# Cross-attention: four buffers of probabilities, V as a ring of tiles, four groups of products with V

## What is computed

```python
k = (key @ Wk.T + bk).reshape(b, lk, H, DH)      # key = value = the context, lk = 1601
v = (value @ Wv.T + bv).reshape(b, lk, H, DH)
q = (query @ Wq.T + bq).reshape(b, lq, H, DH)    # query = layernorm(x), lq = 64
score = jnp.einsum('bqhd,bkhd->bhqk', q, k) / jnp.sqrt(jnp.float32(DH))
...
score = score + jnp.where(valid, 0.0, NEG)[:, None, :, :]
attn = jax.nn.softmax(score, axis=-1)
ctx = jnp.einsum('bhqk,bkhd->bqhd', attn, v).reshape(b, lq, d)
```

## Time and profile before

| | |
|---|---|
| median of 3 runs | 1616.15 us (1612.69 to 1616.39) |
| profiled execution | 1616.18 us, span of its instructions 1614.4 us |
| mean granted TensorE clock | 0.948 of full speed |
| TensorE busy | 1415.4 us, 88% of the span |
| VectorE, ScalarE, GpSimd busy | 1066.6, 900.3, 851.0 us |
| one round of the loop, b = 1 to 29 | 36.32 us |

### The profile page before, as it was taken

The page is one execution under the profiler, slowest core; times in us unless marked ns, Lnnn a source line. Parts: engine busy times, 40 slices in busy tenths (PEclk is TensorE's granted clock), DMA queues, the critical chain, the costliest instruction groups (busy, mean ns, idle before and its releaser), DMA issues. The chain is left out here.

```text
span 1614.4 us, 55265 instructions
## 1 busy us (share of the span) xinstructions
PE 1415.4 (88%) x24351; PEld 983.9 (61%) x24351; DVE 1066.6 (66%) x1681; ACT 900.3 (56%) x1195; POOL 851.0 (53%) x560
## 2 busy tenths in 40 slices
PE   4689999999999999999999999999997686549408
PEld 2357777777767777777767777777775355324107
DVE  7756666666666666666666666666663768785984
ACT  2445566565565566565565566665565565425752
POOL 5567666665555666665555666665530698420000
PEclk9899999999999999999999999999998899679859
DMA  5564444444454444444444444444420521010001
GB/s 169 128 155 105 105 105 114 121 124 113 117 143 106 105 105 114 123 119 116 118 139 107 105 105 112 125 120 114 116 64 25 151 54 28 1 40 0 1 0 53
DMA packets 90495, 155.97 MB, mean 97 GB/s; under 512 B 16704, under 2 KB 55496, under 8 KB 90256
## 3 DMA queue, kind: packets, MB, share of 16 engines
q1 hardware_dynamic: 88256, 150.92, 35.7%
q10 hardware_dynamic: 2000, 1.51, 0.4%
HBM read 60.95 MB, written 2.20 MB: 39 GB/s over the span
## 5 line engine op out<-in xcount | busy, mean ns | idle before, releaser
L638 DVE TENSOR_REDUCE MXP<-W_PS 128x1 f32<-128x512 f32 x768 | 498.9, 687 | 283.8 <-PE W_PS L450 283.8
L534 ACT ACTIVATE PR<-S_PS 128x1024 f32<-128x1024 f32 (+1 forms) x416 | 424.9, 1023 | 259.1 <-PE S_PS L398 251.2
L344 POOL TENSOR_TENSOR K_HI<-K,MCOL 128x512 f16<-128x512 f32 (+1 forms) x224 | 219.5, 980 | 425.7 <-ACT K L542 424.5
L346 POOL TENSOR_TENSOR K_LO<-K,K_HI 128x512 f16<-128x512 f32 (+1 forms) x224 | 291.9, 1303 | 17.6
L450 PE MATMUL W_PS<-STK,QS 105*128 105x512 f16 (+1 forms) x1024 | 269.8, 335 | 8.8 <-POOL STK L371 4.8
L398 PE MATMUL S_PS<-QS,STK 105*128 105x128 f16 (+1 forms) x3328 | 256.1, 220 | 1.0 <-DVE QS L652 1.0
L413 PEld LDWEIGHTS O_PS<-PR,V 128*17 128x17 f32 x13312 | 191.1, 98 | 79.5 <-issue 59.4
L413 PE MATMUL O_PS<-PR,V 128*17 128x64 f32 x13312 | 231.5, 220 | 7.8 <-ACT PR L534 7.5
L433 PE MATMUL W_PS<-WV_HI,CTX_HI 128*128 128x256 f16 (+1 forms) x832 | 228.3, 274 | 1.6 <-DVE WV_LO L611 1.4
L398 PEld LDWEIGHTS S_PS<-QS,STK 105*128 105x128 f16 (+1 forms) x3328 | 201.3, 99 | 44.4 <-DVE QS L652 1.1
L433 PE MATMUL W_PS<-WV_HI,CTX_LO 128*128 128x256 f16 (+1 forms) x832 | 227.8, 274 | 0.0
(11 more groups left out here) (243 smaller groups left out, 1599.0 us busy)
## 6 DMA issues: line engine op xcount, KB each, us to landing
CTX<-in_ctx_t SPq DMA_DIRECT2D x64, 800.5 KB, 5.9
STK<-K_HI SPq DMA_DIRECT2D x256, 128.0 KB, 2.5
STK<-K_HI SPq DMA_DIRECT2D x256, 72.1 KB, 2.1
STK<-K_LO SPq DMA_DIRECT2D x128, 128.0 KB, 2.6
STK<-K_LO SPq DMA_DIRECT2D x128, 72.1 KB, 2.1
QSTK<-STK SPq DMA_DIRECT2D x12, 192.0 KB
SQS<-QK_HI SPq DMA_DIRECT2D x32, 64.0 KB, 2.2
X<-in_x SPq DMA_DIRECT2D x1, 1536.0 KB, 15.7
```

The source lines that it names most:

```text
L344: pool.tensor_tensor(K_HI[:, m, lo:hi], k32, zero, ALU.add).then_inc(k_hi, 1)
L346: pool.tensor_tensor(K_LO[:, m, lo:hi], k32, K_HI[:, m, lo:hi], ALU.subtract).then_inc(k_lo, 1)
L534: nc.scalar.activation(PR[0:m, par, :], S_PS[par][0:m, :], ACT.Exp).then_inc(p_sb, 1)
L638: dve.tensor_reduce(MXP[:, j, at:at + 1], bank[:, :], AX.X, ALU.max).then_inc(mx_done, 1)
```

## The change

PR gets four buffers instead of two, in turn over all tiles of all batches, so an exponential waits for the PV four before it. V becomes one array with room for 11 pairs of tiles, used as a ring: the copy of pair i of batch n waits until the PV of the pair that lay there have been done (`v_free`). The ring of K32 has three buffers instead of four. Some tiles that only the start uses move (XN to PR, KMH to other partitions of V). And SCHEDULE has another order, with the same steps: PV stand in four groups (0 to 3, 4 to 6, 7 and 8, 9 to 12) instead of seven, MX and V begin earlier in a round, OT and CH come later, and K 6 stands last. FIRST is unchanged.

```diff
@@ -61,20 +61,14 @@
 
 
 SCHEDULE = [
-    ("ST", 0), ("QS", 0), ("CH", 0), ("OT", 0), ("V", 0),
-    ("ST", 1), ("V", 1),
-    ("PV", 0), ("PV", 1), ("ST", 2), ("MX", 0), ("MX", 1), ("V", 2), ("MX", 2),
-    ("ST", 3), ("MX", 3), ("V", 3), ("MX", 4), ("MX", 5),
-    ("PV", 2), ("PV", 3), ("ST", 4), ("MX", 6), ("MX", 7), ("V", 4), ("MX", 8),
-    ("ST", 5), ("MX", 9), ("V", 5), ("MX", 10), ("MX", 11),
-    ("PV", 4), ("PV", 5), ("ST", 6), ("MX", 12), ("MX", 13), ("V", 6), ("MX", 14),
-    ("ST", 7), ("MX", 15), ("K", 0), ("MX", 16), ("MX", 17),
-    ("PV", 6), ("PV", 7), ("ST", 8), ("MX", 18), ("MX", 19), ("K", 1), ("MX", 20),
-    ("ST", 9), ("MX", 21), ("K", 2), ("MX", 22), ("MX", 23),
-    ("PV", 8), ("PV", 9), ("ST", 10), ("MX", 24), ("K", 3), ("MX", 25),
-    ("ST", 11), ("K", 4), ("MT", 0),
-    ("PV", 10), ("PV", 11), ("ST", 12), ("K", 5), ("K", 6),
-    ("PV", 12),
+    ("ST", 0), ("V", 0), ("ST", 1), ("QS", 0), ("MX", 0), ("ST", 2), ("MX", 1), ("OT", 0), ("V", 1), ("ST", 3),
+    ("V", 2), ("MX", 2), ("V", 3), ("MX", 3), ("CH", 0), ("MX", 4), ("PV", 0), ("PV", 1), ("PV", 2), ("PV", 3),
+    ("ST", 4), ("MX", 5), ("V", 4), ("MX", 6), ("ST", 5), ("ST", 6), ("MX", 7), ("MX", 8), ("V", 5), ("MX", 9),
+    ("MX", 10), ("PV", 4), ("PV", 5), ("PV", 6), ("MX", 11), ("MX", 12), ("K", 0), ("V", 6), ("MX", 13), ("ST", 7),
+    ("MX", 14), ("K", 1), ("MX", 15), ("K", 2), ("MX", 16), ("MX", 17), ("ST", 8), ("ST", 9), ("MX", 18), ("K", 3),
+    ("MX", 19), ("ST", 10), ("MX", 20), ("ST", 11), ("MX", 21), ("MX", 22), ("PV", 7), ("PV", 8), ("MX", 23),
+    ("ST", 12), ("MX", 24), ("K", 4), ("MX", 25), ("K", 5), ("MT", 0), ("PV", 9), ("PV", 10), ("PV", 11), ("PV", 12),
+    ("K", 6),
 ]
 FIRST = [
     ("V", 0), ("V", 1), ("TN", 1), ("QS", 0), ("MX", 0), ("MX", 1), ("V", 2), ("QY", 1), ("MX", 2), ("MX", 3),
@@ -86,6 +80,9 @@
 BANKED = ("K", "V", "MX", "MT", "OT")
 PER = {k: sum(x[0] == k for x in SCHEDULE) for k in (*BANKED, "ST", "PV")}
 RING = 3
+PR_RING = 4
+K_RING = 3
+V_RING = 11
 OSTEPS = 5
 A_MX = 16
 
@@ -158,11 +155,11 @@
     CTX_LO = alloc("CTX_LO", [P, 2, KT, LK], F16)
     K_HI = alloc("K_HI", [P, KT, LK], F16)
     K_LO = alloc("K_LO", [P, KT, LK], F16)
-    K32 = alloc("K32", [P, 4, CH], F32)
+    K32 = alloc("K32", [P, K_RING, CH], F32)
     STK_MEM = [alloc(f"STK{u}", [P, PAIRS * LK], F16) for u in range(2)]
     STK = [mem[:, :].rearrange("p (j t) -> p j t", j=PAIRS) for mem in STK_MEM]
-    V = [alloc(f"V{u}", [P, NT, H, VW], F32) for u in range(2)]
-    PR = alloc("PR", [P, 2, H * SQ], F32)
+    V = alloc("V", [P, 2 * V_RING, H, VW], F32)
+    PR = alloc("PR", [P, PR_RING, H * SQ], F32)
     QSTK = alloc("QSTK", [P, PAIRS, ROWS], F16)
     QS = alloc("QS", [P, 2, PAIRS, 2, SQ], F16)
     MXP = alloc("MXP", [P, PAIRS, NCH], F32)
@@ -176,12 +173,12 @@
     W_PS = [psum(f"W_PS{i}", [P, 512]) for i in range(RING)]
 
 
-    V1 = V[1][:, :, :, :].rearrange("p t h v -> p (t h v)")
+    V1 = V[:, 2 * PER["V"]:2 * V_RING, :, :].rearrange("p t h v -> p (t h v)")
     TOKI = V1[0:B, 0:LK]
-    KMH = V1[0:B, LK + 1:2 * LK + 1].bitcast(F16)[:, 0:LK]
+    KMH = V1[64:64 + B, 0:LK].bitcast(F16)[:, 0:LK]
     QMR = V1[32:33, 0:ROWS // 2].bitcast(F16)
-    XN = V1[:, 2500:2500 + 4 * D].rearrange("p (a d) -> p a d", a=4)
     PRF = PR[:, :, :].rearrange("p a r -> p (a r)")
+    XN = PRF[:, 2 * KT * CH:2 * KT * CH + 4 * D].rearrange("p (a d) -> p a d", a=4)
     W_RAW = [PRF[:, i * KT * D:(i + 1) * KT * D].rearrange("p (k n) -> p k n", k=KT) for i in range(3)]
     Q32 = [PRF[:, i * KT * CH:(i + 1) * KT * CH].rearrange("p (m r) -> p m r", m=KT) for i in range(2)]
     XT_HI, XT_LO = (STK_MEM[1][:, i * KT * ROWS:(i + 1) * KT * ROWS].rearrange("p (k r) -> p k r", k=KT) for i in range(2))
@@ -218,6 +215,15 @@
 
         if value > 0:
             eng.wait_ge(s, value)
+
+    def v_home(n, i):
+
+        return 2 * ((PER["V"] * n + i) % V_RING)
+
+    def v_free(n, i):
+
+        n, i = divmod(PER["V"] * n + i - V_RING, PER["V"])
+        return NT * n + min(2 * i + 2, NT)
 
     def runs(kind, b):
 
@@ -323,7 +329,7 @@
     @block.gpsimd
     def _(pool):
         pool.memset(MCOL[:, :], 0.0).then_inc(constant, 1)
-        pool.memset(V[0][:, :, :, DH:VW], 1.0).then_inc(constant, 1)
+        pool.memset(V[:, 0:2 * PER["V"], :, DH:VW], 1.0).then_inc(constant, 1)
         ones = float(np.ones(2, np.float16).view(np.float32)[0])
         pool.wait_ge(constant, V_ONES[0])
         pool.memset(STK_MEM[0][ROW_M:ROW_MASK, :].bitcast(F32), ones).then_inc(constant, 1)
@@ -332,7 +338,7 @@
 
             m, lo, hi = k_part(i)
             size = (m.stop - m.start) * (hi - lo)
-            k32 = K32[:, i % 4, 0:size].rearrange("p (m t) -> p m t", t=hi - lo)
+            k32 = K32[:, (PER["K"] * n + i) % K_RING, 0:size].rearrange("p (m t) -> p m t", t=hi - lo)
             pool.wait_ge(k_32, k_written(n, i))
             if i == 0:
                 for c in range(4):
@@ -366,7 +372,7 @@
         body(-1)
         pool.wait_ge(q_first, 16 * 13)
         pool.wait_ge(q_rest, 16 * 13)
-        pool.memset(V[1][:, :, :, DH:VW], 1.0).then_inc(constant, 1)
+        pool.memset(V[:, 2 * PER["V"]:2 * V_RING, :, DH:VW], 1.0).then_inc(constant, 1)
         pool.wait_ge(constant, V_ONES[1])
         pool.memset(STK_MEM[1][ROW_M:ROW_MASK, :].bitcast(F32), ones).then_inc(constant, 1)
         pool.wait_ge(constant, STK_ONES[1])
@@ -400,7 +406,7 @@
                                          start=True, stop=True)
                     last.then_inc(s_ps, 1)
                 elif kind == "PV":
-                    par = (u + i) % 2
+                    at = (NT * b + i) % PR_RING
                     m = P if i < NT - 1 else LAST
                     if i == 0:
                         need(pe, o_sb, b)
@@ -411,7 +417,7 @@
                     for h in range(H):
                         r = 32 * (h % 4)
                         last = pe.matmul(O_PS[r:r + VW, (h // 4) * SQ:(h // 4 + 1) * SQ],
-                                         V[u][0:m, i, h, :], PR[0:m, par, h * SQ:(h + 1) * SQ],
+                                         V[0:m, v_home(b, i // 2) + i % 2, h, :], PR[0:m, at, h * SQ:(h + 1) * SQ],
                                          start=(i == 0 and h < 4), stop=(i == NT - 1), skip_group_check=True)
                     last.then_inc(pv_done, 1)
                 elif kind == "K":
@@ -530,16 +536,16 @@
                     par = (u + i) % 2
                     m = P if i < NT - 1 else LAST
                     act.wait_ge(s_ps, NT * b + i + 1)
-                    need(act, pv_done, NT * b + i - 1)
-                    nc.scalar.activation(PR[0:m, par, :], S_PS[par][0:m, :], ACT.Exp).then_inc(p_sb, 1)
+                    need(act, pv_done, NT * b + i + 1 - PR_RING)
+                    nc.scalar.activation(PR[0:m, (NT * b + i) % PR_RING, :], S_PS[par][0:m, :], ACT.Exp).then_inc(p_sb, 1)
                 elif kind == "K":
                     n = b + 2
                     ms, lo, hi = k_part(i)
                     act.wait_ge(k_ps, PER["K"] * n + i + 1)
-                    need(act, k_lo, PER["K"] * n + i - 3)
+                    need(act, k_lo, PER["K"] * n + i + 1 - K_RING)
                     for s, m in enumerate(range(ms.start, ms.stop)):
                         cols = slice(s * LAST, s * LAST + hi - lo)
-                        nc.scalar.activation(K32[:, i % 4, cols], bank[:, cols], ACT.Identity,
+                        nc.scalar.activation(K32[:, (PER["K"] * n + i) % K_RING, cols], bank[:, cols], ACT.Identity,
                                              bias=BK[:, m:m + 1], scale=1 / W_SCALE).then_inc(k_32, 1)
                 elif kind == "TN":
                     if i == 1:
@@ -552,9 +558,10 @@
                 elif kind == "V":
                     n = b + 1
                     act.wait_ge(v_ps, PER["V"] * n + i + 1)
-                    need(act, pv_done, NT * (n - 1))
-                    t0, t1, m = (2 * i, 2 * i + 2, P) if i < 6 else (12, 13, LAST)
-                    nc.scalar.activation(V[w][0:m, t0:t1, :, 0:DH],
+                    need(act, pv_done, v_free(n, i))
+                    t0 = v_home(n, i)
+                    t1, m = (t0 + 2, P) if i < 6 else (t0 + 1, LAST)
+                    nc.scalar.activation(V[0:m, t0:t1, :, 0:DH],
                                          bank[0:m, 0:(t1 - t0) * D].rearrange("p (t h d) -> p t h d", t=t1 - t0, h=H),
                                          ACT.Copy, scale=1 / W_SCALE).then_inc(v_sb, 1)
             if b >= 0:
```

## The result

| | |
|---|---|
| before | 1615.32 us, median (1612.69 to 1616.39) |
| after | 1599.77 us, median of 4 runs (1597.84 to 1601.88) |
| ratio | 0.9906, 95% interval 0.9886 to 0.9927 |
| forecast | 1581.6 us, range 1572 to 1593 |
| profiled execution of after | 1598.3 us, span 1596.5, mean granted clock 0.947 |

What follows compares the result with a forecast made beforehand. TensorE, busy 88% overall and nearly always in the loop, was taken as the bound. Savings of 29.3 - 1.0 + 1.3 + 5.0 = 34.6 us from 1616.2 gave 1581.6 us, range 1572 to 1593.

Steps and rivals of the forecast that it cites:

- first round: First batch: MX 0 waits for the memset with less work under it, +2.9; memset 1.1 earlier, groups save; net +1.0 us.
- 29 full rounds: Cross-attention loop: each full batch takes 35.31 instead of 36.32 us, 1.01 less, 29.3 us saved in all.
- second to last: Second to last batch, which has no K: saves the 1.01 and shorter last waits for exponentials, 1.3 us.
- last round: Last batch: idle between S_PS banks comes only behind PV 3 and PV 6 instead of six times, 5.0 us saved.
- Long PV groups run dry: Rival: PV beyond the second of a group cost more as instruction feeding fails; 28 us, 1609, chance 5%.
- after the 64th of a group: Sign of being wrong: the spacing of PV matmuls grows after the 64th matmul of a group.
- Three groups fewer: Each batch: PV in four groups instead of seven saves 3 x 0.22 = 0.66 us of entering and leaving.
- OT: Each batch: OT moved back no longer waits for the copy of the outputs to OSB, 0.22 us saved.
- two banks: Each batch: two small waits for a work bank, at MX behind V 6 and K 2, go; 0.13 us saved.
- Exits into MX: Leaving a PV group into MX taken at 0.12 us, as into ST; rival of dearer exits 1590 to 1601, 8%.
- The rings: Waits from four probability buffers, eleven V pairs and three fp32 K buffers, costed at nothing.
- CTX_LO: GpSimd's CTX_LO ends 0.4 to 0.8 us ahead of K 0, no wait; rival that it comes late: 1621, 5%.

Runs made afterwards that it cites:

- r3: Changed kernel, order untouched, TensorE's program aligned ahead of MX 15 at place 104 of a 256-instruction block; 1574.57 us, ratio 0.9753.
- r2: Changed kernel with PV in five groups of at most three, CH moved up by a few steps; 1586.46 us, ratio 0.9825.
- r1: All rings of the change, but the order of steps of the kernel before, with seven PV groups; 1614.23 us, ratio 0.9998.
- r8: Kernel before with one step moved: OT behind V 1 instead of right behind QS and CH; 1815.77 us, ratio 1.1246.
- r10: Kernel before with OT and then CH both moved behind V 1; 1653.01 us, ratio 1.0236.
- r6: Kernel before, with only TensorE's program aligned ahead of MX 15 at place 104 of a block; 1690.31 us, ratio 1.0467.
- r9: Kernel before, TensorE's program aligned ahead of MX 15 at place 0 of a block instead of 104; 1711.36 us, ratio 1.0582.

## Why the prediction was too good

By its own steps, with the kernel whose edges lie apart (r3) beside after. ST 0 of each round is the mark; all in us of span:

```
                              forecast   after    of this to stops   r3
start, to ST 0 of b = 0          0       +1.35                      +2.34
first round                     +1.0     +1.36         1.8          -0.44
29 full rounds                 -29.3    -16.5         15.6         -32.1
second to last                  -1.3     +0.20         1.7          -1.46
last round                      -5.0     -2.7          2.3          -4.97
behind the loop                  0       -1.6                       -1.4
sum                            -34.6    -17.9         21.4         -38.1
```

**The step that failed** is the rival "Long PV groups run dry", held at 5% and costed at nothing in the sum, on the ground that "both halves of a pair see 36 weight loads in the same 0.44 us, so the second PV is fed as fast as the first". That row answers a question about the feeding from matmul to matmul, and its answer was right: in a clean group of four, start to start is 1.91 us, with no slower second half. But a pair is 128 instructions and the supply comes by 256. No stretch of the old order could show a block used up in 1.9 us; what was there to see was the row of q8 on the page (16 KB a packet), and one stop of 0.38 us in the kernel before, at the end of a block of 5.8 us, whose next packet began only 3.8 us after the block was entered. The prediction has neither:

```profile
q8 instruction: 193, 3.16, 0.8%
...
920.04 0.97 PE L413 MATMUL O_PS<-PR,V 128*17 128x64 f32 x54
921.17 0.38 PE L413 MATMUL O_PS<-PR,V 128*17 128x64 f32 x10 [0.16 <-issue]
```

The prediction's own test, the spacing "after the 64th of a group", would have found 4 of the 13 stops; the other nine stand ahead of the ST, V or K behind a group. So the rival named the right place for the wrong reason: it thought of a queue that a long group empties, at the same price in each round, where it is the edge of a block, in 13 rounds of 29. Its price was 28 us; it was 21.4 (the third column: what after took more than r3, half clock behind a stop included). After the longest stop in the full rounds the clock fell too (busy time by stretch; the third column from the end is the granted clock):

```profile
925.60:929.10 3.50, 3.50 (x31) 2.89 (x30) 0.00 (x0) 1.82 (x4) 0.83 (x2) 0.51 0.67 149
```

**Three groups fewer, OT, two banks: 1.01 a round.** Right in sum: 36.32 to 35.23 is 1.09. The group's price is shown by itself: r2 has one group more and 0.23 us more. Exits into MX cost 0.12, as taken. Of the 0.08 left over I have no share for each step, and the 0.22 of OT and the 0.13 of the banks are not shown one by one.

**Costed at nothing.** The rings: right, by r1. CTX_LO: 0.38 us ahead of K 0, at the near end of the 0.4 to 0.8 worked out, and no wait. ScalarE stood up to 0.7 us a round for PV 7, where about a microsecond was said, and no engine felt it. But OT and CH, which the forecast moved freely, are not free to move: r8 and r10 cost 200 and 39 us. That VectorE's part of OT is over before CTX_LO begins, and that the cast stands where MX can wait for it, is cover that the prediction didn't name, and the changed order happens to keep it.

**The first round.** MX 0 waited 6.12 us, against 4.83 before and 6.6 by the forecast's terms (4.83 + 2.9 - 1.1), and the half clock stayed, as said:

```profile
96.05 5.43 POOL L377 MEMSET STK<- 8x6404 f32 x1
```

```profile
101.73 0.58 PE L456 MATMUL W_PS<-STK,QS 105*128 105x512 f16 x1 [6.12 <-POOL STK L377]
```

The memset ended 8.25 us behind ST 0, in the kernel before 10.27: 2.0 us earlier, where 1.1 was costed. After's +1.36 looks like the +1.0 forecast, but isn't: 1.7 of it is one stop at K 6, at the edge of a block, and without it the round is shorter than before, as in r3 (-0.44). The term was 1.4 us too dear, 0.9 of it by the memset.

**The last two rounds.** Without stops -1.46 and -4.97 for -1.3 and -5.0: right.

**Start and tail.** Costed at 0, they moved by +1.35 and -1.6. The clock at the start rose at 28.0 us instead of 26.2, which I can't trace to the change: of the kernels in the old order, r1 has the same start as before (92.0), r6 and r8 have 92.5 and r10 has 93.1.

With the stops away the forecast would have been 3.5 us too long: 1576.3 is r3's span, 1579.8 the one forecast (1614.4 - 34.6). By the medians it is 7.0 (1574.57 against 1581.6), still inside the range.

## What to carry to other kernels

Ask of every dense stretch not only what each instruction needs, but how fast it uses up instructions: here 256 of TensorE's that were gone in 2 to 4 us could meet the edge of a block before the next one was there, and a row of a shorter stretch cannot show that. Where a kernel runs near this, split the dense stretch, or choose by alignment where the edges fall, then look at the first edge behind the jump. And before a step is moved, list what the other engines do at its new place: one small addition of VectorE's beside a long operation of GpSimd's cost 6 us here.

## What the runs showed of the hardware

- A stop at a block's edge needs no full clash: a block with 102 of 128 PV matmuls (3.0 us) stopped, and in r2 three of 3.5 to 4.1 us; longer ones nearly never (0.38 us in the kernel before and 0.19 in r1, both behind blocks of 5.8 us, where the packet began 3.8 and 3.6 us after the block was entered). Packets of 16 KB took 0.88 to 1.72 us in after, and in after, r6 and r9 TensorE went on 1.0 to 1.6 us after their end.
- A jump in TensorE's program was free in r3 (35.23 with it and without), where it came 210 instructions into a block and 6.5 us of work followed. It cost stops of 2.1 us a round with 3.1 us of work behind it (r6), and of 2.3 us where it came 106 instructions into a block (r9); with the half clock behind them the rounds were 2.7 and 3.2 us longer.
- A 64x256 addition on VectorE out of SBUF took 0.42 us alone, 0.67 beside one of GpSimd's K_HI, and 5.7 or 6.1 when it began after a CTX_LO of GpSimd's had. The Trainium skill (Perfetto Trace Analysis, Optimizing Scalar/DVE Operations) has the two engines share a read port that an operation of VectorE's can hold to itself; in r8 it was VectorE that waited, for all of an operation of GpSimd's that had begun first.
- After the stop of 1.97 us the granted clock was 0.51 for about 3.5 us; after those of up to 1.64 us in the full rounds of after it stayed at 1.00.
